# Attention inside a fused transformer block: maxima in two turns, the output projection over four units, its root on VectorE, and a lag of seven slots

## The reference

```
x = x + layernorm(attention(layernorm(x)))      # 16 heads of 32, causal, softmax, then @ Wo
x = x + layernorm(ffn(layernorm(x)))            # 512 -> 2048 -> 512, sine terms, relu
scores  = q k^T + causal mask, divided by sqrt(512)
weights = softmax(scores);  out = (weights @ v) @ Wo
layernorm(y) = (y - mean) / sqrt(var + 1e-5)
```

## Time and profile before

| | |
|---|---|
| runs shown | 3408.65, 3409.79, 3410.0 us; median 3409.79 us |
| the profiled execution | 3411.96 us, span 3410.2 us |
| granted TensorE clock, mean of the span | 0.977 |
| first phase, attention, feed-forward | about 0 to 600, 600 to 2036, 2036 to 3410 us |

### The profile page before, as it was taken

How to read it: one execution, slowest core, us unless ns; L and a number is a source line. 1 busy time by engine, 2 the same in 40 slices (tenths; PEclk the granted TensorE clock), 3 DMA queues, 4 the chain that set the end, 5 groups by cost and what they waited for, 6 DMA issues and landing times. The chain is left out here.

```text
span 3410.2 us, 76837 instructions
## 1 busy us (share of the span) xinstructions
PE 3194.2 (94%) x29988; PEld 1862.5 (55%) x29988; DVE 2246.6 (66%) x4217; ACT 2066.2 (61%) x2451; POOL 1324.5 (39%) x703
## 2 busy tenths in 40 slices
PE   6999998899899898989899979999999999999998
PEld 3444443666667676767666754444444444444443
DVE  5655455777777676767677745666666666666665
ACT  2323332988979797979798855555555555555554
POOL 1000000898979797989798960000000000000000
PEclk8999999999999999999999989999999999999999
DMA  4564852122222222222222231000000000000000
GB/s 139 183 216 146 246 188 95 46 65 80 66 84 63 85 59 88 66 79 67 76 77 73 66 110 57 25 25 25 25 25 25 25 25 25 25 25 25 25 25 25
DMA packets 193086, 246.67 MB, mean 72 GB/s; under 512 B 15936, under 2 KB 134912, under 8 KB 190592
## 3 DMA queue, kind: packets, MB, share of 16 engines
q1 hardware_dynamic: 192768, 242.24, 22.6%
HBM read 148.87 MB, written 92.80 MB: 71 GB/s over the span
## 5 line engine op out<-in xcount | busy, mean ns | idle before, releaser
L1338 POOL TENSOR_TENSOR a_prob_lo<-a_prob,a_prob_hi 128x2048 f16<-128x2048 f32 (+2 forms) x448 | 1191.8, 2690 | 175.8 <-ACT a_prob_hi L1244 174.3
L297 DVE TENSOR_REDUCE u_mx<-a_pw 128x4 f32<-128x512 f32 (+1 forms) x1178 | 730.0, 657 | 157.6 <-PE a_pw L283 118.8
L1234 ACT ACTIVATE a_prob<-a_pst,a_lift,w_exp_scale 128x1024 f32<-128x1024 f32 (+1 forms) x640 | 709.2, 1123 | 198.5 <-PE a_pst L1171 101.9
L1244 ACT ACTIVATE a_prob_hi<-a_prob 128x2048 f16<-128x2048 f32 (+2 forms) x448 | 583.4, 1302 | 0.0
L1655 ACT ACTIVATE f_hidden_work<-f_ph,w_turn,w_fold 128x512 f32<-128x512 f32 x256 | 199.1, 778 | 586.2 <-PE f_ph L1701 585.7
L1701 PE MATMUL f_ph<-f_xT,f_w 128*128 128x512 f16 x2304 | 528.7, 380 | 0.0
L1722 PE MATMUL f_py<-f_w,f_act 128*128 128x512 f16 x2280 | 523.3, 380 | 0.2
L1198 PE MATMUL a_acc<-u_vt,a_prob_hi 128*128 128x33 f16 x9216 | 466.5, 179 | 47.0 <-POOL a_prob_lo L1338 26.8
L1198 PEld LDWEIGHTS a_acc<-u_vt,a_prob_hi 128*128 128x128 f16 x9216 | 432.9, 97 | 127.8 <-DVE a_o L1275 27.9
L1171 PE MATMUL a_pst<-u_qp,u_kp 98*128 98x256 f16 (+1 forms) x2560 | 463.9, 267 | 37.4 <-issue 21.6
L215 POOL TENSOR_TENSOR s_ve<-s_mv,s_eps 128x4 f32<-128x4 f32 x31 | 8.8, 285 | 1245.6 <-DVE s_mv L201 1245.6
(11 more groups left out here) (182 smaller groups left out, 4031.8 us busy)
## 6 DMA issues: line engine op xcount, KB each, us to landing
qk_parts<-q_stage SPq DMA_DIRECT2D x128, 256.0 KB, 3.5
u_qp<-qk_parts SPq DMA_DIRECT2D x192, 128.0 KB, 2.7
u_kp<-qk_parts SPq DMA_DIRECT2D x192, 128.0 KB, 2.8
v_parts<-q_vstage SPq DMA_DIRECT2D x16, 1056.0 KB, 5.3
u_vt<-v_parts SPq DMA_DIRECT2D x32, 528.0 KB, 4.3
q_x<-in_L_attn_h_dram SPq DMA_DIRECT2D x16, 1024.0 KB, 10.2
q_raw<-in_L_ffn_W_dram SPq DMA_DIRECT2D x16, 1024.0 KB, 8.2
u_xr<-in_L_attn_h_dram SPq DMA_DIRECT2D x64, 256.0 KB, 3.0
```

What stands on the lines that cost most here:

```text
L297: dve.tensor_reduce(out, src[:, 0:n * len(heads)].rearrange("p (h n) -> p h n", n=n), AX_X, ALU.max).then_inc(units.released, 1)
L1234: act.activation(prob[:, k % PR, :, off:QC], pst[:, k % 2, :, off:QC], ACT.Exp, scale=exp_scale, bias=lift[:, :]).then_inc(exp_done, 1)
L1244: act.activation(prob_hi[:, first % HR:first % HR + steps, :, off:QC], prob[:, first % PR:first % PR + steps, :, off:QC], ACT.Copy).then_i ...
L1338: pool.tensor_tensor(prob_lo[:, first % HR:first % HR + steps, :, off:QC], prob[:, first % PR:first % PR + steps, :, off:QC], prob_hi[:, f ...
```

## The change

- **Maxima in two turns.** The pieces of the next unit lie in slots 3 to 19 (32 of them, `NEXT_AT`), and its last 6 in its own slots 0 to 2 (`OWN_AT`). The maxima of the first 512 queries are turned in slot 12 and stored; those of the second 512 in the unit's own slot 3, for which its slot 6 waits (`SECOND_HALF_AT`). Each turn has its own two DMAs of half the size. Tiles `qp`, `mx` and `nm` are laid out by halves.
- **Output projection.** `WO_AT` becomes 11, 19, ... 67, eight slots apart, over four units. DVE's `wo_out` comes 6 slots after a tile's start, not 4. `oT` gets a fifth group, used for group 0 in odd batches.
- **Root.** POOL's two instructions go. DVE computes 1/sqrt in 8 `tensor_scalar` steps on a 128x1 float32 tile (an estimate by integer arithmetic, two refinements), one every half slot, or all in one slot for the last batch.
- **LAG** is 7, not 6, so that every weighing, normalising and turn comes a slot later.
- **Loop.** The hardware loop has 3 passes of two batches each, not 6 of one.
- **End of the first phase.** SP's `first_units` issues 3 loads at each of two places in chunks 10 to 13, not 12 at once; the pieces of the first unit end with two turns of maxima.

```
-LAG = 6
+LAG = 7
-PIECES_AT = dict(enumerate((3, 3, 3, 3, 2, 2, 1, 2, 2, 3, 2, 2, 3, 2, 2, 3)))
-MAX_AT = 17
+NEXT_AT = dict(enumerate((1, 2, 2, 2, 1, 3, 1, 3, 2, 3, 1, 3, 2, 2, 1, 2, 1), 3))
+OWN_AT = {0: 2, 1: 2, 2: 2}
+MAX_EARLY_AT, MAX_LATE_AT = 12, 3
-WO_AT = list(range(10, 10 + 5 * QT, 5))
-WO_AT_LAST = [10, 15, 20, 21, 25, 26, 28, 29]
+WO_AT = list(range(11, 11 + 8 * QT, 8))
+WO_AT_LAST = [11, 16, 21, 22, 26, 27, 29, 30]
-WO_STATS, WO_SMALL, WO_OUT, WO_STORE = 2, 2, 4, 5
+WO_STATS, WO_OUT, WO_STORE = 2, 6, 7
+LAST_OUT, LAST_STORE = 3, 4
+ROOT_STEPS = 8
+ROOT_AT = {(2, 1): (0,), (3, 0): (1,), (3, 1): (2,), (4, 0): (3,), (4, 1): (4,), (5, 0): (5,), (5, 1): (6,), (6, 0): (7,)}
...
-                    if part < 2:
-                        for c in range(CPB):
-                            load_qk(sp, units, qk_parts, 0, part, c, True)
-                            load_qk(sp, units, qk_parts, 0, part, c, False)
+                    part = 2 * (n - LOAD_CHUNK) + (m == 6)
+                    if part < 2 * 2 * CPB:
+                        load_qk(sp, units, qk_parts, 0, part // (2 * CPB), part // 2 % CPB, part % 2 == 0)
...
+            if self.this and (u > 0 or self.before):
+                n = sum(NEXT_AT.values()) + sum(OWN_AT.get(kk, 0) for kk in range(k))
+                out += [(u, k, "piece", u, m) for m in range(n, n + OWN_AT.get(k, 0))]
+            if self.this and (u > 0 or self.before) and k == MAX_LATE_AT:
+                out.append((u, k, "max", u, 1))
...
-                run(0, FIRST)
-                with engine.Fori(1, BATCH - 1) as i:
-                    run(i, MIDDLE)
-                run(BATCH - 1, LAST)
-                run(BATCH, DRAIN)
+                run(0, FIRST, 0)
+                with engine.Fori(0, BATCH // 2 - 1) as pair:
+                    run(2 * pair + 1, MIDDLE, 1)
+                    run(2 * pair + 2, MIDDLE, 0)
+                run(BATCH - 1, LAST, 1)
+                run(BATCH, DRAIN, 0)
...
-                        if k == 0:
-                            pe.wait_ge(nm_stored, 32 * v + 32)
+                        if k in (0, SECOND_HALF_AT):
+                            pe.wait_ge(nm_stored[int(k > 0)], 32 * v + 32)
...
+                    if step == 0:
+                        dve.wait_ge(mv_done, n + 1)
+                        dve.tensor_scalar(v, mv[:, t % YR, 1:2], eps, None, ALU.add).then_inc(root_step, 1)
+                        return
+                    dve.wait_ge(root_step, ROOT_STEPS * n + step)
+                    if step == 1:
+                        dve.tensor_scalar(y0.bitcast(I32), v.bitcast(I32), -0.5, float(ROOT_BITS), ALU.mult, ALU.add
+                                          ).then_inc(root_step, 1)
+                    elif step == 2:
+                        dve.tensor_scalar(h0, y0, y0, v, ALU.mult, ALU.mult).then_inc(root_step, 1)
...
-                    pool.tensor_tensor(small[:, s, 0:1], mv[:, s, 1:2], eps, ALU.add).then_inc(small_done, 1)
-                    pool.wait_ge(small_done, 2 * n + 1)
-                    pool.tensor_tensor(small[:, s, 1:2], small[:, s, 0:1], half[:, :], ALU.pow).then_inc(small_done, 1)
```

More of the change, by code:

```diff
@@ L535, in _ @@
                 sp.wait_ge(v_stored, 16 * NCH + START)
-                sp.wait_ge(units.nm_stored, 32)
+                for half in range(CPB):
+                    sp.wait_ge(units.nm_stored[half], 32)
             @block.gpsimd
@@ L945, in tiles, with last_batch @@
                 yield -1, m
+    def last_batch(self, b):
+        return (b == 0 and self.this and not self.after) or not self.this
     def shared_work(self):
@@ L1021, in attention_phase @@
         mv = sb("mv", [P, YR, 2])
[L1022 to L1023 removed]
+        root = sb("root", [P, YR, ROOT_STEPS])
         y = feed.xin[:, 1]
@@ L1095, in run @@
                             load_qk(sp, units, qk_parts, i, u + 2, 0, False)
-                        for b, t in stage.tiles(u, k, WO_STORE):
+                        stored = [(b, t) for b, t in stage.tiles(u, k, WO_STORE) if not stage.last_batch(b)]
+                        stored += [(b, t) for b, t in stage.tiles(u, k, LAST_STORE) if stage.last_batch(b)]
+                        for b, t in stored:
                             sp.wait_ge(y_done, QT * (i + b) + t + 1)
@@ L1113, in run @@
                                          ).then_inc(feed.b2_loaded, 16)
[L1114 to L1118, removed]
+                        for at, what, unit, half in stage.at(u, k):
+                            if what == "max":
+                                sp.wait_ge(released, work_before(i, stage) + at + 1)
+                                store_max(sp, units, unit % 2, half)
                 run_all(sp, run)
@@ L1134, in shared @@
                     elif what == "max":
-                        pe.wait_ge(max_ready, UNITS * i + unit + 1)
-                        last = turn_maxima(pe, units, pw[:, bank])
+                        if m == 0:
+                            early = next(n for n, it in enumerate(stage.work)
+                                         if it[2:] == ("piece", unit, FIRST_OF_SECOND - 1))
+                            pe.wait_ge(released, before + early + 1)
+                        else:
+                            pe.wait_ge(max_ready, UNITS * i + unit + 1)
+                        last = turn_maxima(pe, units, pw[:, bank], m)
                     else:
@@ L1205, in _, with run @@
                 PARTS = 2 + TQ
-                def run(i, stage):
+                def run(i, stage, parity):
                     before = work_before(i, stage)
@@ L1301, in wo_out, with roots @@
                                              ALU.add).then_inc(y_done, 1)
-                def shared(i, at, before, what, unit, m, stage):
+                def roots(i, stage, u, k, late):
+                    for (lag, end), steps in ROOT_AT.items():
+                        for b, t in stage.tiles(u, k, lag):
+                            if end == late and not stage.last_batch(b):
+                                for step in steps:
+                                    wo_root(i + b, t, step)
@@ L1314, in run @@
                             wo_stats(i + b, t, stage)
+                            if stage.last_batch(b):
+                                for step in range(ROOT_STEPS):
+                                    wo_root(i + b, t, step)
+                        roots(i, stage, u, k, 0)
                         for at, what, unit, m in stage.at(u, k):
-                            shared(i, at, before, what, unit, m, stage)
+                            shared(i, at, before, what, unit, m, stage, parity)
                         e = stage.earlier(u, k, LAG)
@@ L1357, in run @@
                             deviations(pool, feed, 0, 1)
-                        for b, t in stage.tiles(u, k, WO_SMALL):
-                            wo_small(i + b, t)
                 pool.memset(feed.half[:, :], -0.5).then_inc(feed.const, 1)
```

154 lines of the change are left out of this document (93 added, 61 removed).

## The result

The changed kernel takes 3363.58 us (median of 4, 3361.18 to 3366.36), the kernel before 3409.22 on the same chip: a ratio of 0.9866, interval 0.9849 to 0.9884, 45.6 us faster. The forecast was 3304 us. The profiled execution took 3365.03 us with a span of 3363.1 us.

The account below looks back on a forecast made before the run. ACT and POOL were taken to bound units without projections, PE or its waits the others. Terms summed to -106 us from the profiled 3411.96: 3306 us, or 3304 against the median; range of 8 in 10: 3252 to 3364 us.

Parts of the forecast that it names:

- rival 1: Attention units: the spread brings nothing, PE still pays a tile's full price; 42.5 to 43.7 us a unit, 3374 us; chance 0.18.
- batches 1 to 6: Main attention loop: 24 units of 40.6 us plus jumps and entry, 984.5 us for 1071.8, -87.3 us.
- last batch: Last attention batch: three units of 40.6 us plus one of 39.5, 161.3 us for 172.0, -10.7 us.
- I take 1.05 us a tile, so 40.6 us a unit: Attention units with two projection tiles: cost above the free unit's 38.5 us; bounds 38.5 and 43.7 us a unit.
- The working itself: Slot sums for a tile: about 0.8 us in slots 7, 8, 15, 16; 1.5 to 2.5 us in 19, 0, 3, 4, 11, 12.
- It is not the bound: DVE in attention units: with 2.5 us of root steps it is busy 34.9 us of 40.6.
- costs one slot in the drain: LAG 7: PE weighs a step later, so POOL may be later before PE stalls; price one slot in the drain.
- The loop: Jumps back of the hardware loop: five before, two after, 3 x 4.3 = -12.9 us.
- the loads: First phase, chunks 10 and 11: three loads at a time fit between stores, -9.5 us; bounds -10 and -5.
- The drain: After the last exponential: chained root steps on DVE plus the slot of LAG, +2 us; bounds 0 and +6.
- The root waiting for POOL's access: Rival at each `tensor_scalar` of `wo_root`: DVE blocked by POOL's SBUF access, slower, 470 us more, 3770 us; chance 0.05.
- The late store: Rival at slot 6: second store of maxima late, 0 to 1.5 us a unit, at 1.5 3350 us; chance 0.04, 0.01 slower.

Follow-up runs that it names:

- projection_third: Changed kernel with 4 of a tile's 12 projection products, the low-part passes left out: 3289.56 us, ratio 0.9654 to the kernel before.
- pieces_moved: Changed kernel with pieces of slots 8 and 12 cut to one each, the others moved, early turn of maxima in slot 13: 3337.80 us.
- lag_6: Changed kernel with LAG 6 in place of 7 and tiles one slot earlier: 3334.27 us, ratio 0.9775 to the kernel before.
- lag_6_pool: Changed kernel with LAG 6, tiles one slot earlier and the root back on POOL: 3328.26 us, ratio 0.9766 to the kernel before.
- root_on_pool: Changed kernel with the root back on POOL, output still six slots behind a tile's start: 3334.90 us, ratio 0.9788 to the kernel before.
- pieces_moved_pool: Changed kernel with one piece each in slots 8 and 12, early turn in slot 13, and the root on POOL: 3299.67 us, ratio 0.9677.
- loop_alone: Kernel before with only the loop changed, to 3 passes of two batches: 3392.62 us, ratio 0.9957.
- tiles_alone: Kernel before with the two-batch loop and tiles eight slots apart; LAG 6, old pieces, root on POOL: 3505.57 us, ratio 1.0276.

## Why the prediction was wrong in size

**The sign** was right, and rival 1 (a unit of 43.2, 3374 us) named what came, with a chance of 0.18. The 3363.58 us lie at the very end of the range of 8 in 10 (3252 to 3364). Against the profiled execution the steps come out so:

| step | forecast | measured |
|---|---|---|
| first phase with its end | -8.5 | -13.3 |
| first batch | -1.5 | +0.6 |
| batches 1 to 6 | -87.3 | -34.3 |
| last batch | -10.7 | -6.7 |
| drain | +2 | +7.4 |
| next phase | 0 | -0.9 |
| sum | -106 | -47.2 |

The spans differ by 47.1 us; the rest is rounding.

**The step that failed** is "I take 1.05 us a tile, so 40.6 us a unit". With the 10.1 us that the forecast had for jumps and entry set aside, a unit of batches 1 to 6 takes (1037.5 - 10.1) / 24 = 42.8 us; against the 38.5 of a unit without tiles that is 4.3 / 2 = 2.15 us a tile, twice the value taken. It makes 2.2 us a unit, 53 us on 24 units. The first three units of the last batch add 8 (130.2 us for 3 x 40.6): 61 us against the 59 that the sum is off, and the other rows cancel to -2.

The base was off too. The changed kernel's own units without tiles take 39.1 us, not 38.5 (36.8 with the pieces moved); by them a tile costs 3.7 / 2 = 1.85 us. That fits the products: 24 at the 0.16 us of `projection_third` are 3.8 us, if all weigh as the 16 did. The parts don't add up, though. The root (0.7 us a unit), half the reducing (2.2) and the order of the pieces (0.8) each bring something beside it, and in `pieces_moved` the difference is 42.0 - 36.8 = 5.2 us, the full price of two tiles again. There the units without tiles gained 2.3 us, those with tiles 0.8.

The working itself was nearer. Of a batch's eight tiles three start in slot 7 or 15, which it put at 0.8 us, and five in 19, 3 or 11, at 1.5 to 2.5: a mean of 1.2 to 1.9 us. The value taken lay below that, because the sum over the unit left PE slack and it took off "what PE was ahead". That PE's time over in one slot can't be saved for a later one, with scores two steps deep and two banks for pieces, is argued; what the runs show is that less work for PE and less for DVE both shorten a unit in which each has time over.

**"It is not the bound"**, said of DVE, holds for its sum over a unit, and a unit still answers to DVE. Its load rose from 777.85 us to 839.69 us in batches 1 to 6, near the 2.5 us a unit that was worked out, and the root cost 0.7 us a unit though DVE stood idle for 8 of the 43.2 us (839.69 / 24 = 35.0 busy). Nor was the place of the divisions seen: LAG 7 "costs one slot in the drain", said the forecast, but it also moves normalising into slots 8 and 12, each with three pieces. In the units without tiles LAG 6 with the same pieces is 1.7 us shorter, as shown above. In those with tiles `pieces_moved` gains 0.4 us each at slots 8 and 9 and 1.1 at slot 12, and gives 1.1 back in others; how much of slot 12 is the early turn, which moved too, was not separated.

**LAG 7** takes away PE's waits for POOL's low parts, but in both pairs of runs that differ in it (and in the tiles' slots) LAG 6 is the faster: 3334.27 against 3363.58 us, and 3328.26 against 3334.90 with the root on POOL. `lag_6` and the root on POOL don't add (29 and 29 alone, 35 together). Of the 23 us that are missing, 15 lie in batches 1 to 6, 10 of them at slot 2 (1.71 us in the changed kernel, 1.89 in `lag_6`, 2.28 with both), where PE waits for low parts in `lag_6_pool` alone (6.7 us of 29.7 in all slots); 7 lie in the last batch and the drain. That POOL's root makes these low parts late is likely and was not traced.

**The loop** was right (14.2 alone for 12.9), and **the loads** (8.7 for 9.5). In the changed kernel the first phase gave 13.3 by the traces. The four traces in which it is unchanged have the first exponential at 599.0 to 602.1 us, so that of the 13.3 some 3 us can be scatter of the kernel before.

**The drain** looks mis-sized, +7.4 for +2, outside its bounds of 0 to +6. But the forecast also put the last unit at 39.5 us, and it took 35.1. The last unit and the drain together went from 72.9 to 75.9 us, +3.0 for +2: two errors that cancel, which is luck. DVE's timeline there:

```profile
1967.53 0.21 DVE L1344 TENSOR_SCALAR a_root<-a_mv,w_wo_eps 128x1 f32<-128x1 f32 x1
...
1969.27 0.21 DVE L1364 TENSOR_SCALAR a_root<-a_root 128x1 f32<-128x1 f32 x1
1969.40 0.69 DVE L1331 BATCH_NORM_STATS2 a_stats<-a_pst 128x6 f32<-128x512 f32 x1
```

```profile
1948.87 10.53 DVE L221 TENSOR_SCALAR s_work<-s_x,s_mv,s_rstd 128x512 f32<-128x512 f32 x4
1959.32 0.74 DVE L1371 SCALAR_TENSOR_TENSOR s_x<-a_pwo,a_root,u_xr 128x512 f32<-128x512 f32 x1
```

Eight steps take 1.95 us (1967.53 to past 1969.27), near the 1.7 forecast. Six tiles are left in the drain, 11.7 us of DVE, which is the busiest engine there: 32.10 of 40.78 us. `root_on_pool` has a drain of 30.5 us and a last unit of 38.2, in all 7.3 us less; but its four normalisations also took 7.09 us in place of 10.53 (see the last section), so that not all of this is the root's. The forecast thought the steps partly hidden beside PE's products. Why the last unit became shorter was not traced.

**The root waiting for POOL's access** did not come. The first and the longest of its steps, over all 64 tiles:

```profile
L1344 DVE TENSOR_SCALAR a_root<-a_mv,w_wo_eps x64: 202/204/215, 733.2 to 1986.0; 128x1 f32<-128x1 f32 x64
...
L1351 DVE TENSOR_SCALAR a_root<-a_root x64: 264/265/274, 736.3 to 1986.5; 128x1 f32<-128x1 f32 x64
```

No step took over 0.274 us while POOL was busy 894.87 of 1037.54 us. The Trainium skill (VectorE: DVE Perf Modes, "What auto-detection actually checks") puts one-source operations between SBUF tiles in the two-port mode by their outermost non-unit sizes. Read as the forecast read it, that takes in these steps, and with its rule on the shared access they would block; the trace does not agree. A step of 128x1 has no such size within a partition, so the rule may not be meant for it. **The late store** costs next to nothing; what the score products (L1212) waited for from 590 to 1949 us, with the times and the number of waits:

```profile
  ACT a_prob L1275: 70.7, 129
  issue: 14.2, 14
  DMA u_qp<-u_nm: 6.2, 9
```

The DMA is at most 6.2 us in all the attention, 0.2 us a unit.

## What to carry to other kernels

Where an engine's queue is in order and its buffers hold only two steps, don't add up a unit: add up the larger of the engines' times slot by slot, with every wait for a bank in it, and take that sum and not a value below it. Moving the same work to other slots was worth 26 us here, more than the loop (14.2) and the loads (8.7) together, and spreading one stage without giving its consumer later slots cost 119. Measure a stage together with its neighbour before calling either of them longer or shorter. A short operation costs by where it stands: chained on the engine that ends the drain it is paid in full, and in a queue of 4-us instructions it is late for whoever waits.

## Not expected of the hardware

The normalisation of 128x512 float32 from SBUF to SBUF on DVE took 10.53 us for four beside POOL's low parts (9.15 before) and held the first tile of the drain, so that PE waited 7.83 us. All 64 instructions of this form in the changed kernel (ns min/median/max), POOL's low parts beside the first four, the same four in `pieces_moved_pool`, and PE's wait:

```profile
L221 DVE TENSOR_SCALAR s_work<-s_x,s_mv,s_rstd x64: 540/543/4278, 1948.9 to 3229.3; 128x512 f32<-128x512 f32 x64
...
1947.29 11.82 POOL L1426 TENSOR_TENSOR a_prob_lo<-a_prob,a_prob_hi 128x2048 f16<-128x2048 f32 x4
```

```profile
1892.97 2.13 DVE L221 TENSOR_SCALAR s_work<-s_x,s_mv,s_rstd 128x512 f32<-128x512 f32 x4
```

```profile
1960.12 2.32 PE L1197 MATMUL a_pwo<-w_wo,a_oT 128*128 128x512 f16 x5 [7.83 <-DVE s_x L1371]
```

The other 60 run in the feed-forward part, where POOL stands still, and take 0.54 us each. The four beside POOL take 2.78, 4.28, 2.34 and 1.37 us, and each ends 0.3 us after one of POOL's four instructions ends. In `pieces_moved_pool` three of the four fall into a pause of POOL, and the four take 2.13 us together. So the time beside POOL is waiting and not work, some 8 us on the path of the drain. This agrees with the rule of the Trainium skill that such an operation and a GpSimd one block each other (SBUF — State Buffer, "SBUF: two separate sides").

The granted clock in batches 1 to 6 was 0.97 in the kernel before, 0.98 in `loop_alone`, 0.99 in the changed kernel, and 0.93 in `tiles_alone`, where PE stands most.
